# A decoder's two 32-head attentions: the out products of two batches as 7 products of parts

## The reference

```python
queries = rope((x @ Wq.T))       # 32 heads of 128
keys    = rope((ctx @ Wk.T))     # 8 heads of 128, each shared by 4 query heads
values  =       ctx @ Wv.T       # 8 heads of 128
attn = softmax(queries @ keys.T * 128 ** -0.5 + mask)
x = layernorm(x + concat(attn @ values) @ Wd.T)    # Wd.T: 4096 x 512
```

## Time and profile before

| | |
|---|---|
| median of three runs | 2843.52 us |
| profiled execution | 2848.45 us, span 2847.1 us |
| mean granted TensorE clock | 0.981 |
| TensorE busy, matmuls | 2702.1 us (95%) |
| VectorE busy | 1579.9 us (55%) |
| ScalarE busy | 773.7 us (27%) |
| GpSimd busy | 382.2 us (13%) |
| out products L628 | 463.1 us busy, 1024 records |
| projections L589 from xT | 457.9 us busy, 1024 records |
| additions L731 | 87.1 us busy, 128 |

### The profile page before, as it was taken

How to read it: one execution, slowest core, us unless ns; L and a number is a source line. 1 busy time by engine, 2 the same in 40 slices (tenths; PEclk the granted TensorE clock), 3 DMA queues, 4 the chain that set the end, 5 groups by cost and what they waited for, 6 DMA issues and landing times.

```text
span 2847.1 us, 38391 instructions
## 1 busy us (share of the span) xinstructions
PE 2702.1 (95%) x15096; PEld 1649.8 (58%) x15096; DVE 1579.9 (55%) x2793; ACT 773.7 (27%) x2502; POOL 382.2 (13%) x455
## 2 busy tenths in 40 slices
PE   8989999999998889899999999998998898999998
PEld 7855555555555566555555555556774455566664
DVE  3555556555556577455655555565766653344455
ACT  0012222222233233112222222322332512333331
POOL 1021111111112100121111111122111031000002
PEclk9999999999999899999999999999999999999999
DMA  8630110110000100001011010010000020000000
GB/s 178 92 124 22 38 37 23 38 37 15 15 15 37 67 2 2 27 23 37 23 37 38 16 37 15 15 67 31 2 2 27 1 81 27 14 22 4 12 1 30
DMA packets 53811, 94.75 MB, mean 33 GB/s; under 512 B 29408, under 2 KB 38560, under 8 KB 47488
## 3 DMA queue, kind: packets, MB, share of 16 engines
q1 hardware_dynamic: 53632, 92.30, 10.7%
HBM read 83.89 MB, written 8.39 MB: 32 GB/s over the span
## 4 chain that ended last, share of the span: by engine, by line
PE 89%; DVE 7%; issue 1%; ACT 1%; DMA 1%; POOL 1%; SPq 0%; DVEq 0%; POOLq 0%; ACTq 0%
PE banks L589 19%; PE banks L628 16%; PE banks L608 4%; PE banks L638 4%; PE banks L581 4%; PE banks L1578 3%; PE banks L1068 3%; PE banks L303 3%; PE banks L1630 3%; PE banks L1900 2%; PE banks L1868 2%; PE banks L1933 2%; PE banks L1607 2%; PE banks L1583 2%; PE banks L618 2%; PE banks L1646 2%
## 5 line engine op out<-in xcount | busy, mean ns | idle before, releaser
L628 PE MATMUL banks<-weights,OT 128*128 128x512 f32 x1024 | 463.1, 595 | 5.9 <-DMA weights<-in_L_xwo 5.4
L589 PE MATMUL banks<-xT,weights 128*128 128x512 f32 x1024 | 457.9, 592 | 0.0
L664 ACT ACTIVATE E_x<-S_x,sm_x 128x128 f32<-128x128 f32 x512 | 199.2, 390 | 545.9 <-DVE sm_x L717 545.9
L589 PEld LDWEIGHTS banks<-xT,weights 128*128 128x128 f32 x1024 | 189.1, 190 | 210.4 <-issue 210.4
L697 DVE TENSOR_TENSOR turned<-banks,const 64x512 f32<-64x512 f32 x160 | 109.4, 684 | 357.2 <-PE banks L589 357.1
L628 PEld LDWEIGHTS banks<-weights,OT 128*128 128x128 f32 x1024 | 185.1, 191 | 191.6 <-issue 184.5
L746 POOL TENSOR_TENSOR QT<-QT,turned 128x512 f32<-128x512 f32 x128 | 162.1, 1266 | 787.1 <-DVE QT L699 787.1
L1989 ACT ACTIVATE E_s<-banks,top_s 128x128 f32<-128x128 f32 x512 | 138.9, 382 | 291.2 <-DVE top_s L2086 291.2
L161 POOL TENSOR_TENSOR norm_spread<-norm_mv,const 128x1 f32<-128x1 f32 x96 | 20.7, 216 | 1229.0 <-DVE norm_mv L157 1229.0
L726 DVE TENSOR_TENSOR E_x<-E_x,sm_x 128x512 f32<-128x512 f32 x128 | 179.4, 1401 | 4.4
L678 ACT ACTIVATE OT<-banks 128x512 f32<-128x512 f32 x128 | 76.4, 597 | 386.6 <-PE banks L638 386.6
(11 more groups left out here) (281 smaller groups left out, 4089.5 us busy)
## 6 DMA issues: line engine op xcount, KB each, us to landing
weights<-in_L_xwq SPq DMA_DIRECT2D x16, 1024.0 KB, 4.9
weights<-in_L_xwo SPq DMA_DIRECT2D x16, 1024.0 KB, 4.9
weights<-in_L_xwk SPq DMA_DIRECT2D x16, 256.0 KB, 5.2
weights<-in_L_xwv SPq DMA_DIRECT2D x16, 256.0 KB, 5.4
weights<-in_L_ffn_W_base SPq DMA_DIRECT2D x3, 1024.0 KB, 5.0
weights<-in_L_xwq SPq DMA_DIRECT2D x4, 768.0 KB, 5.0
weights<-in_L_xwo SPq DMA_DIRECT2D x4, 768.0 KB, 5.7
xT<-in_xT SPq DMA_DIRECT2D x4, 512.0 KB, 9.9
```

The lines of the kernel that those rows point to most:

```text
L589: mm = PE.matmul(bank[:, :], weight, source[:, k, half_of(i)], start=k == 0, stop=k == KC - 1)
L628: mm = PE.matmul(psum[7][:, :], OT[u % 2][:, h, :], wo[:, h, :], start=h == 0, stop=h == 3)
L664: ins = AC.activation(e[:, j, :], s[:, j, :], ACT.Exp, bias=sm[:, 0, j:j + 1], scale=1.0, accum_out=sm[:, 1, j:j + 1])
```

## The change

The products of two batches (256 rows) with a group's wo (512 x 512) are cut into 2 x 2 parts: rows by batch, heads (0, 1 | 2, 3), columns (0 to 255 | 256 to 511). Instead of 8 products of parts 7 are made (P1 to P7), after Winograd's form: VectorE makes 4 sums of parts of OT for each pair of batches (`ot_sums`, 128x256 each), GpSimd 4 sums of parts of wo for each group (`wo_sums`, 128x512 each, between the rotations of jobs 6 and 7 of the next group). The products stand in four turns over two steps, (P1, P2) and (P6, P4) in the even step, (P7, P5) and (P3) in the odd one, in banks 6 and 7. VectorE adds them to x in 6 operations, two of them of 512 columns of output and four of 256. The first turn of a step stands where the out product stood, ahead of the mix; the second turn stands after job part 1. Of the 64 units the last two keep the old form, later in the step. The mix moves to bank 5 and the transposes keep only bank 4. OT holds two batches in each of its two buffers.

`wo` gets a second buffer in columns that the other arena leaves free, and SP loads group g's once the products of the groups up to g - 2 are over.

Group 1's jobs 0 and 1 (its keys) are made ahead of the loop. Group 0's plan becomes `(0, 2, 2, 2, 2, 1, 1, 0)`.

Normalised batches turn by `normed_at`; batch 6 turns after the loop.

```diff
@@ -476,7 +476,8 @@
 G8 = 8
-xwqkv_in, xwo_in = [signal(f"cross_wqkv_in{n}", 16) for n in range(2)], signal("cross_wo_in", 16)
+xwqkv_in, xwo_in = [signal(f"cross_wqkv_in{n}", 16) for n in range(2)], [signal(f"cross_wo_in{n}", 16) for n in range(2)]
+xwo_sums, x_ot_sums = signal("cross_wo_sums"), signal("cross_ot_sums")
@@ -494,20 +495,24 @@
+    rest = arenas[1 - stage % 2][:, 9240 - 5120:9240]
     views = {name: [a.place(P, KC * n).rearrange("p (k n) -> p k n", k=KC) for _ in range(2)] for name, n in (("wq", D), ("wk", P), ("wv", P))}
-    views["wo"] = a.place(P, 4 * D).rearrange("p (k n) -> p k n", k=4)
+    views["wo"] = [t.rearrange("p (k n) -> p k n", k=4) for t in (a.place(P, 4 * D), rest[:, 0:4 * D])]
+    views["wo_sums"] = rest[:, 4 * D:8 * D].rearrange("p (s k n) -> p s k n", s=4, k=2)
+    views["ot_sums"] = rest[:, 8 * D:10 * D].rearrange("p (s k n) -> p s k n", s=4, k=2)
...
         load_cross_qkv(layer, views, g)
-    SP.dma_start(views["wo"], dram[f"{layer}_xwo"][0]).then_inc(*xwo_in.one())
+    SP.dma_start(views["wo"][0], dram[f"{layer}_xwo"][0]).then_inc(*xwo_in[0].one())
...
     norm = Norm((0, 1))
-    wo = views["wo"]
+    wo, WS, OS = views["wo"], views["wo_sums"], views["ot_sums"]
     units = B * G8
-    qkv_base, wo_base = [s.count - 48 for s in xwqkv_in], xwo_in.count - 16
+    qkv_base, wo_base = [s.count - 48 for s in xwqkv_in], [xwo_in[0].count - 16, xwo_in[1].count]
@@ -517,19 +522,21 @@
         PT = [sbuf(f"PT{n}_{stage}", [P, 4, P], scope) for n in range(2)]
-        OT = [sbuf(f"OT{n}_{stage}", [P, 4, P], scope) for n in range(2)]
+        OT = [sbuf(f"OT{n}_{stage}", [P, 2, 4, P], scope) for n in range(2)]
...
         order = (0, 1, 4, 5, 2, 3, 6, 7, 8, 9, 10, 11)
-        plan = (2, 2, 2, 2, 2, 1, 1, 0)
...
+        plans = [(0, 2, 2, 2, 2, 1, 1, 0)] + [(2, 2, 2, 2, 2, 1, 1, 0)] * (G8 - 2)
...
                 return []
-            first = sum(plan[:b])
+            plan = plans[g]
+            first = NJ - sum(plan[b:])
@@ -553,15 +560,44 @@
+        pairs = units // 2 - 1
+        turns = (("P1", "P2"), ("P6", "P4"), ("P7", "P5"), ("P3",))
+        NT, NA, added_at = len(turns), 6, (0, 2, 3, 5)
...
+        def turn_at(step, part):
...
+            q = (step - 4) // 2
+            return [(q, 2 * (step % 2) + part)] if 0 <= q < pairs else []
...
+        def plain_at(step):
+            u = step - 3
+            return u if 2 * pairs <= u < units else None
...
+        def outs(q):
...
+            return NT * q
...
+        def wo_here(g):
+            return xwo_in[g % 2].sem, wo_base[g % 2] + 16 * (g // 2 + 1)
...
+        normed_at = {units - 2: (0,), units - 1: (1,), units: (2,), units + 1: (3,), units + 2: (4, 5)}
...
                     load_cross_qkv(layer, views, g + 2)
+                if g == 1:
+                    SP.wait_ge(*before.added)
+                if g >= 2:
+                    SP.wait_ge(*x_out(outs(4 * (g - 1))))
                 if g:
-                    SP.wait_ge(*x_out(B * g))
-                    SP.dma_start(wo, dram[f"{layer}_xwo"][g]).then_inc(*xwo_in.one())
+                    SP.dma_start(wo[g % 2], dram[f"{layer}_xwo"][g]).then_inc(*xwo_in[g % 2].one())
@@ -589,6 +625,36 @@
+            def products(q, turn):
+                g = q // 4
+                if turn == 0:
+                    PE.wait_ge(*wo_here(g))
+                    PE.wait_ge(*x_ot(2 * q + 2))
+                if turn == 1:
+                    PE.wait_ge(*xwo_sums(g + 1))
+                    PE.wait_ge(*x_ot_sums(q + 1))
+                if NA * q + added_at[turn]:
+                    PE.wait_ge(*x_sum(NA * q + added_at[turn]))
+                for name in turns[turn]:
+                    mm = product(q, name)
+                mm.then_inc(*x_out.one())
...
+            def product(q, name):
+                o, w = OT[q % 2], wo[q // 4 % 2]
+                left, right = {
+                    "P1": (o[:, 1, 0:2, :], w[:, 0:2, 0:HALF // 2]),
+                    "P2": (o[:, 1, 2:4, :], w[:, 2:4, 0:HALF // 2]),
+                    "P3": (OS[:, 3], w[:, 2:4, HALF // 2:HALF]),
+                    "P4": (o[:, 0, 2:4, :], WS[:, 3]),
+                    "P5": (OS[:, 0], WS[:, 0]),
+                    "P6": (OS[:, 1], WS[:, 1]),
+                    "P7": (OS[:, 2], WS[:, 2])}[name]
+                first = name in ("P1", "P2", "P4", "P5")
+                to = psum[7 if name in ("P1", "P6", "P7") else 6][:, 0:HALF // 2]
+                for k in range(2):
+                    mm = PE.matmul(to, left[:, k, :], right[:, k, :], start=first and k == 0, stop=k == 1, skip_group_check=name in ("P6", "P7", "P3"))
+                return mm
@@ -596,6 +662,8 @@
                 job(0, i)
+            for i in range(2):
+                job(1, i)
@@ -612,21 +680,13 @@
                     PE.wait_ge(*x_prob(u + 1))
-                    if u >= 2:
-                        PE.wait_ge(*x_pt(u - 1))
+                    if u:
+                        PE.wait_ge(*x_pt(u))
                     for h in range(4):
-                        mm = PE.transpose(psum[4 + u % 2][:, rows_of(h)], E[u % 3][:, h, :], ident)
+                        mm = PE.transpose(psum[4][:, rows_of(h)], E[u % 3][:, h, :], ident)
                     mm.then_inc(*x_pturn.one())
-                if step >= 3:
-                    u = step - 3
-                    if u % B == 0:
-                        PE.wait_ge(xwo_in.sem, wo_base + 16 * (u // B + 1))
-                    PE.wait_ge(*x_ot(u + 1))
-                    if u:
-                        PE.wait_ge(*x_sum(u))
-                    for h in range(4):
-                        mm = PE.matmul(psum[7][:, :], OT[u % 2][:, h, :], wo[:, h, :], start=h == 0, stop=h == 3)
-                    mm.then_inc(*x_out.one())
+                for j in turn_at(step, 0):
+                    products(*j)
@@ -635,11 +695,21 @@
                         PE.wait_ge(*x_ot(u))
-                    PE.matmul(psum[6][:, :], V[g % 2][:, b, :], PT[u % 2][:, :, :], start=True, stop=True).then_inc(*x_mix.one())
+                    PE.matmul(psum[5][:, :], V[g % 2][:, b, :], PT[u % 2][:, :, :], start=True, stop=True).then_inc(*x_mix.one())
...
                     job(*j)
-                if step >= units - 4:
-                    norm.turn(step - (units - 4))
+                for j in turn_at(step, 1):
+                    products(*j)
+                u = plain_at(step)
+                if u is not None:
+                    PE.wait_ge(*x_ot(u + 1))
+                    PE.wait_ge(*x_sum(NA * pairs + u - 2 * pairs))
+                    for h in range(4):
+                        mm = PE.matmul(psum[7][:, :], OT[u // 2 % 2][:, u % 2, h, :], wo[(G8 - 1) % 2][:, h, :], start=h == 0, stop=h == 3)
+                    mm.then_inc(*x_out.one())
+                for b in normed_at.get(step, ()):
+                    norm.turn(b)
+            norm.turn(B - 2)
@@ -671,16 +741,17 @@
                         AC.wait_ge(*x_mix(u - 1))
-                    AC.activation(PT[u % 2][:, :, :], four(psum[4 + u % 2][:, :]), ACT.Copy).then_inc(*x_pt.one())
+                    AC.activation(PT[u % 2][:, :, :], four(psum[4][:, :]), ACT.Copy).then_inc(*x_pt.one())
                     AC.wait_ge(*x_mix(u + 1))
-                    if u >= 2:
-                        AC.wait_ge(*x_out(u - 1))
-                    AC.activation(OT[u % 2][:, :, :], four(psum[6][:, :]), ACT.Copy).then_inc(*x_ot.one())
+                    if u >= 4 and u % 2 == 0:
+                        AC.wait_ge(*x_out(outs(u // 2 - 1)))
+                    AC.activation(OT[u // 2 % 2][:, u % 2, :, :], four(psum[5][:, :]), ACT.Copy).then_inc(*x_ot.one())
...
                         value_copy(*j)
-                if step >= units - 4:
-                    norm.copy(step - (units - 4))
+                for b in normed_at.get(step, ()):
+                    norm.copy(b)
+            norm.copy(B - 2)
@@ -698,12 +769,44 @@
+            def ot_sums(q):
+                o = OT[q % 2]
+                DV.wait_ge(*x_ot(2 * q + 2))
+                if q:
+                    DV.wait_ge(*x_out(outs(q)))
+                a11, a12, a21, a22 = o[:, 1, 0:2, :], o[:, 1, 2:4, :], o[:, 0, 0:2, :], o[:, 0, 2:4, :]
+                DV.tensor_tensor(OS[:, 0], a21, a22, ALU.add)
+                then(DV.tensor_tensor(OS[:, 2], a11, a21, ALU.subtract))
+                then(DV.tensor_tensor(OS[:, 1], OS[:, 0], a11, ALU.subtract))
+                DV.tensor_tensor(OS[:, 3], a12, OS[:, 1], ALU.subtract).then_inc(*x_ot_sums.one())
...
+            def add(q, turn):
...
+                b = 2 * q % B
+                low, high = slice(0, HALF // 2), slice(HALF // 2, HALF)
+                first, second = psum[7][:, low], psum[6][:, low]
+                upper, lower = x[:, b + 1, :], x[:, b, :]
+                both = x[:, b:b + 2, :].rearrange("p b (c n) -> p (b c) n", c=2)[:, 0::3, :]
+                adds = (((upper[:, low], first), (upper[:, low], second)),
```

(56 more changed lines are left out.)

## The result

The changed kernel took 2913.86 us (median of 4 runs, 2911.60 to 2919.97) against 2844.68 us before (4 runs): a ratio of 1.0248, 95% interval 1.0236 to 1.0260, or +69.2 us. The profiled execution took 2912.22 us, its span is 2910.9 us.

A forecast was written before the change was run, and what follows sets the result against it. It took TensorE, busy for 2702.1 of 2847.1 us, as the bound. Terms -51.5 + 111.7 - 5.4 + 0 + 6 = +60.8, with +27 by the clock, gave +88: 2931 us from the median 2843.52, range 2880 to 2975.

The forecast's parts named there:

- rival A: TensorE's clock holds through the new short waits: +53 us, 2896 us; chance 0.25.
- the term for the clock: TensorE's clock falls after half of 58 new waits: +27 us, bounds -8 (none) and +96 (all).
- Products removed: TensorE's out products, 7 in place of 8: 0.83 us saved a pair, 62 pairs, -51.5 us.
- Waits at b = 5 and 6: TensorE's second turn waits for VectorE's additions behind the division: 2.29 and 2.02 us, 30.2 us a stage.
- Wait before the mix without a job: At b = 7 and in the last group, TensorE waits 1.71 us for the PT copy, 25.7 us a stage.
- No waits at b = 0 to 4: In two-job steps the second job covers VectorE's additions before TensorE's second turn: costed at nothing, 0.8 us to spare.
- GpSimd's sums at nothing: GpSimd's four sums of wo a group, 5.1 us, delay nothing; upper bound 1.3 us per group, 21 us.
- rival D: GpSimd's run holds VectorE's division back as a whole at b = 3: +59 us, 2990 us; chance 0.04.
- wo's second buffer: The wait for wo in each stage's last group, 2.77 and 2.65 us, goes: -5.4 us.
- the start even: Group 1's early keys turn 5.36 us of starting waits into about 5.2: nothing, bounds -7 and +6.
- the end +6: Later last units and a shared bank at each stage's end add some 3 us a stage: +6, bounds 0 and +12.
- rival B: TensorE's clock falls after nearly every new wait: +157 us, 3000 us; chance 0.12.

The follow-up runs named there:

- x1: The changed kernel with VectorE's additions of the first turn put ahead of the division in steps with one job: 2860.89 us, ratio 1.0052.
- x4: x2 with the single job of b = 5 and 6 moved from part 0 to part 1, between mix and second turn: 2830.57 us, ratio 0.9949.
- x2: The changed kernel with ScalarE's PT copy put ahead of the exponentials in steps without a job in part 0: 2884.81 us, ratio 1.0143.
- z1: The kernel before, old products, plus wo's second buffer, early keys, and PT copy ahead of exponentials in steps 2, 3 and without jobs: 2821.38 us, 0.9924.

## Why the prediction was right

It forecast 2931 us in a range of 2880 to 2975, slower, +88; measured were 2913.86, +69, halfway between the forecast and rival A (2896). The mechanism, two waits for VectorE's additions at b = 5 and 6 and one for the PT copy in steps without a job, is the one that the runs show; the term for the clock was mis-sized. Point by point:

- **Products removed, -51.5.** Right: L655 in x8 takes 1.89 - 0.38 = 1.51 for 7 distances, 0.216 us.
- **Waits at b = 5 and 6.** 2.29 and 2.02 forecast, 2.28 and 2.12 measured, 14 times each. x1 shortened them to 0.55 and 0.38 and x4 removed them at that place, by two different changes of order.
- **Wait before the mix without a job.** 1.71 forecast, 1.67 measured in 27 of 30 (the other three are shown as 1.16, 1.87 and 1.88 in place of 1.50); x2 removed it by ScalarE's order alone.
- **No waits at b = 0 to 4.** Right for the groups from 1 on; in group 0 there is one of 0.3 us a stage. VectorE's four sums of OT take 0.41 to 0.43 us each, but for 2 of the 248, which took 1.53 and 1.50.
- **GpSimd's sums at nothing.** Right for TensorE, and rival D is out. GpSimd itself lost 0.45 us in the first of its four sums, beside VectorE's division (1.72 in place of 1.27):

```profile
609.19 1.77 DVE L834 TENSOR_TENSOR E_x<-E_x,sm_x 128x512 f32<-128x512 f32 x1
...
610.38 1.72 POOL L861 TENSOR_TENSOR weights<-weights 128x512 f32<-128x512 f32 x1
```

- **wo's second buffer -5.4, the start even, the end +6.** Right in sign. The waits at the end were 0.91, 0.39, 0.61, 0.44 and 1.29 us, where I had 0.3, 0.5, 0.7, 0.6 and 1.6; those at the start 3.71 and 0.69, where I had 4.1 and 0.9.
- **The clock.** This step failed in its size. I took +27 from "half of the 58 new waits" at 1.2 us each. By the granted clock, 7 of the 58 were followed by a stretch at 1.2 GHz, all behind waits of 2.1 or 1.9 us and none behind the 30 before the mix. The seven stretches are 23.9 us long, which costs 12 us where I had 35. The start keeps 10.2 us at half clock. Together that is 34.0 us against 17.0: +8.5. This is such a stretch, behind the wait at b = 5 of another group; scores take 1.83 us where they took 1.05:

```profile
364.39 1.13 PE L655 MATMUL banks<-weights 128*128 128x256 f32 x4 [2.11 <-DVE x L798]
365.36 1.83 PE L676 MATMUL banks<-KT,QT 128*128 128x128 f32 x8
```

- **What the account left out:** 4.5 to 7 us of slower first records behind waits, and -9.4 us of luck in stages 2 and 3.
- **Slips in its sums.** All 58 waits at 1.7 us less 8 are +91 and not +96, so rival B is 2995. The point where the change wins before the clock is at 25 of the 56 us of waits a stage and not at 28. Neither moves the forecast.

With 8.5 in place of 27 the forecast's own sum is 2844 + 60.8 + 8.5 = 2913. That this is the measured time to 1 us is luck: the two items left out nearly cancel, since the -9.4 is counted from a profiled execution that lay 4.9 us above its median.

The section of the Trainium skill that I weighed, "A second HAM failure mode: psum-queue depth-cycling" on the page TensorE: Matmul & The Clock Gate, made the upper bound the nearer one. The measurement decides against that bound for this kernel: 51 of 58 short waits left the clock at its upper level, though the clock did fall behind 7. The other, on the page SBUF — State Buffer, section "SBUF: two separate sides", agrees with the 1.77 us of the division beside GpSimd (0.69 alone) and the 1.72 us of GpSimd beside the division (1.27 alone). The loss that it made me weigh for the sums of OT came in 2 of 248.

## What to carry to other kernels

Cutting one long instruction group into turns with a hand-over between engines can take away more than it saves when the group was the cover of another chain. Before such a change list what the long group hid, here 3.44 us of out product over a copy behind exponentials and an addition behind a division, and give each its cover back or move it in its own engine's queue. A wait in a fixed order is often cured by moving one instruction of an engine with room. Here four such moves (the PT copy without a job and at the start, the single job, P3) and the old form in the last group turned +2.5% into -1.6%. Of the -1.6%, somewhat over half is the 7 products; the rest is the second buffer of wo, the early keys and the start, as z1 shows (-0.8%). Where no other work can cover the turns, as in a last group, keep the old form.

## What was not expected of the hardware

The lower level of TensorE's clock came far less often behind short waits than six older rows suggested: 7 of 28 behind waits of 1.94 to 2.12 us, 0 of 30 behind 1.16 to 1.88. Waits of one length had both outcomes, and what decides between them no run here shows. And the two stages 2 and 3, whose code is the same, took 307.2 to 316.6 us in the kernels of this document, with mean granted clocks of 0.95 to 0.92: a difference of under 10 us in the whole can come from there, so the change's own stages are the better measure.
